# Moved words in the hand-written engine orders of a self and cross attention block

## What is computed

```python
attn_in = _adaln(x, cond, ln1_w, ln1_b, g1_w, g1_b, b1_w, b1_b)
x = _attn(attn_in, attn_in, sa_wq, sa_wkv, sa_wo, sa_bo) + x
cross_in = _adaln(x, cond, ln1_w, ln1_b, g1_w, g1_b, b1_w, b1_b)
ctx_n = _ln(context, ca_lnc_w, ca_lnc_b)
x = _attn(cross_in, ctx_n, ca_wq, ca_wkv, ca_wo, ca_bo) + x
ffn_in = _adaln(x, cond, ln2_w, ln2_b, g2_w, g2_b, b2_w, b2_b)
h = jax.nn.gelu(ffn_in @ ff_w1 + ff_b1, approximate=False)
x = h @ ff_w2 + ff_b2 + x
```

## Time and profile before

| | |
|---|---|
| times of three runs | 1933.48, 1933.77, 1937.64 us |
| the profiled execution, span of its instructions | 1934.6 us |
| TensorE (PE) busy | 1889.5 us, 98% |
| its weight loads (PEld) busy | 1289.2 us, 67% |
| VectorE (DVE) busy | 1582.3 us, 82% |
| GpSimd (POOL) busy | 1266.3 us, 65% |
| ScalarE (ACT) busy | 945.2 us, 49% |
| chain that ended last | PE 87%, POOL 4%, issue 3%, DVE 3% |

### The profile page before, as it was taken

How to read it: one execution, slowest core, us unless ns; L and a number is a source line. 1 busy time by engine, 2 the same in 40 slices (tenths; PEclk the granted TensorE clock), 3 DMA queues, 4 the chain that set the end, 5 groups by cost and what they waited for, 6 DMA issues and landing times.

```text
span 1934.6 us, 52084 instructions
## 1 busy us (share of the span) xinstructions
PE 1889.5 (98%) x19952; PEld 1289.2 (67%) x19952; DVE 1582.3 (82%) x2316; ACT 945.2 (49%) x1460; POOL 1266.3 (65%) x816
## 2 busy tenths in 40 slices
PE   7999999979999999999999999999999999999999
PEld 5666767745666666666666666666666666666664
DVE  4999999967888888888888888888888888888842
ACT  3555545533545444445554445455444445544444
POOL 4777756415776676677767677776776667667661
PEclk8999999978999999999999999999999999999999
DMA  5332233211111111111111111111111111111100
GB/s 176 117 88 86 81 112 88 73 33 48 53 54 53 55 51 53 59 55 54 54 51 55 52 58 57 51 56 51 55 50 56 57 54 56 51 53 52 53 29 23
DMA packets 147729, 119.07 MB, mean 62 GB/s; under 512 B 63392, under 2 KB 111648, under 8 KB 147488
## 3 DMA queue, kind: packets, MB, share of 16 engines
q1 hardware_dynamic: 110624, 115.46, 17.9%
q10 hardware_dynamic: 36864, 0.28, 1.0%
HBM read 36.71 MB, written 1.05 MB: 20 GB/s over the span
## 4 chain that ended last, share of the span: by engine, by line
PE 87%; POOL 4%; issue 3%; DVE 3%; DMA 1%; ACT 1%; SPq 0%; ACTq 0%; DVEq 0%; POOLq 0%
PE S L1376 24%; PE OB L1390 20%; PE PB L1338 10%; PE PB L1325 10%; PE S L1357 7%; PE PB L1399 2%; PE PB L1310 2%; PE S L1225 2%; PE PB L1409 1%; PE PB L1191 1%; PE OB L1253 1%; PE OB L1236 1%; DMA swapped<-turned 1%; POOL KL L667 1%; POOL psum_acc L674 1%
## 5 line engine op out<-in xcount | busy, mean ns | idle before, releaser
L708 POOL TENSOR_TENSOR psum_acc<-psum_acc,P 124x1024 f32<-124x1024 f32 (+1 forms) x320 | 689.8, 2156 | 216.9 <-ACT P L851 207.4
L851 ACT ACTIVATE P<-S 124x1024 f32<-124x1024 f32 (+1 forms) x448 | 431.3, 963 | 514.6 <-PE S L1376 513.9
L1069 DVE TENSOR_REDUCE mxc<-S 128x2 f32<-128x1024 f32 x384 | 470.0, 1224 | 94.9 <-PE S L1357 88.1
L1390 PE MATMUL OB<-P,V 124*64 124x256 f32 (+1 forms) x3328 | 437.3, 387 | 0.0
L1390 PEld LDWEIGHTS OB<-P,V 124*64 124x64 f32 (+1 forms) x3328 | 221.4, 137 | 188.7 <-issue 104.8
L701 POOL TENSOR_TENSOR psum_acc<-P 124x1024 f32<-124x1024 f32 x64 | 152.0, 2374 | 213.4 <-ACT P L851 213.4
L1376 PE MATMUL S<-QH,KH 64*124 64x256 f32 (+1 forms) x1664 | 271.8, 323 | 5.8 <-ACT P L851 5.8
L728 ACT ACTIVATE V<-PB 124x512 f32<-124x512 f32 (+1 forms) x320 | 157.2, 491 | 206.4 <-PE PB L1338 167.0
L1376 PEld LDWEIGHTS S<-QH,KH 64*124 64x124 f32 (+1 forms) x1664 | 154.0, 181 | 128.5 <-issue 104.7
L1376 PE MATMUL S<-QL,KH 64*124 64x256 f32 (+1 forms) x1664 | 235.2, 278 | 0.0
L1376 PE MATMUL S<-MX,share 64*124 64x256 f32 (+1 forms) x1664 | 235.0, 278 | 0.0
(11 more groups left out here) (159 smaller groups left out, 2844.8 us busy)
## 6 DMA issues: line engine op xcount, KB each, us to landing
swapped<-turned SPq DMA_DIRECT2D x512, 128.0 KB, 2.1
kv_w<-sa_kv_dram SPq DMA_DIRECT2D x64, 128.0 KB, 2.3
qswapped<-qturned SPq DMA_DIRECT2D x128, 64.0 KB, 1.9
kv_w<-ca_kv_dram SPq DMA_DIRECT2D x64, 96.0 KB, 2.2
ctxT_all<-ctx_dram SPq DMA_DIRECT2D x8, 624.0 KB, 4.4
q_w<-sa_wq_dram SPq DMA_DIRECT2D x64, 64.0 KB, 2.0
q_w<-ca_wq_dram SPq DMA_DIRECT2D x64, 64.0 KB, 2.0
o_w<-ca_wo_dram SPq DMA_DIRECT2D x64, 64.0 KB, 2.0
```

The source lines that it names most:

```text
L708: pool.tensor_tensor(acc, acc, P_of(J, c)[0:rows, :, 0:w], ALU.add).then_inc(x.acc, 1)
L851: act.activation(P_of(J, c)[0:rows, :, 0:w], SP[0:rows, :, 0:w], ACT.Exp, scale=SCALE).then_inc(x.e, 1)
L1069: dve.tensor_reduce(mxc[:, t, :, c:c + 1], MP[:, :, 0:w], AX.X, ALU.max).then_inc(x.am, 1)
L1390: ins = pe.matmul(OB[half(h), 0:N], Vb[J % 2][0:w, t, half(h)], P_of(J, c)[0:w, h, k * N:(k + 1) * N], start=(t == 0), stop=(t == len(a_.t ...
```

## The change

Only the order strings change; every instruction is there as before.

```diff
--- before.py
+++ after.py
@@ -81,20 +81,19 @@
     CTX = B * M + 56
     TOK = CTX - B * CW
     SELF = Stage("sa",
-                 "qk+3 ln+3 o+-2 p+-1 sum+-1 v+2 s a+2 ct n",
-                 "c+2 ln+2 am+1 ad+-2 r+2 t+3 rc+-1 dv+-1 cn n",
-                 "mr+1 ve+2 e ca cn ln+3 h+3 oe",
-                 "f cp l+3 cc+3 cq",
-                 "w+4 x+3")
+                 "qk+3 ln+3 o+-2 p+-1 sum+-1 v+2 a+2 s ct n",
+                 "c+2 ln+2 cn+-1 am+1 ad+-2 r+2 t+3 rc+-1 dv+-1 n",
+                 "ve+2 mr+1 e ca cn ln+3 h+3 oe",
+                 "cp l+3 f+1 cc+3 cq",
+                 "w+5 x+3")
     CROSS = Cross("ca", DC, M, 124, 512,
-                  "a4 k1+1 p2+-1 v3+-1 a5 n0 s4+-1 q+1 p3+-1 a6 s5+-1 p4+-1 v0 k2+1 n1 p5+-1 s6+-1 a0+1 v1 n2 s0 "
-                  "a1+1 p6+-1 k3+1 v2 n3 s1 a2+1 sum+-1 k0+2 n4 s2 a3+1 p0 p1 o+-1 s3",
-                  "am4 kc0+1 kt1+1 am5 qt+1 ka0+1 am6 qc+1 kl0+1 nm n0 kc1+1 ka1+1 kt2+1 kc2+1 n1 am0+1 kl1+1 ka2+1 am1+1 "
-                  "kl2+1 kt3+1 am2+1 kc3+1 rc+-1 dv+-1 ka3+1 am3+1 kl3+1 ad+-1 kt0+2",
-                  "e1+-1 e2+-1 kh3 e3+-1 ve3+-1 e4+-1 kh0+1 e5+-1 mr ve0 n0 qh+1 e6+-1 kh1+1 ve1 n1 e0 kh2+1 ve2 "
-                  "oe+-1 n2",
-                  "c4+-1 qa+1 c5+-1 cf+-1 c6+-1 ql+1 c1 c2 c3",
-                  "w+2 k0+1 k1+1 q+1 wo k2+1 k3+1")
+                  "a4 k1+1 p2+-1 v3+-1 a5 n0 s4+-1 q+1 p3+-1 a6 s5+-1 p4+-1 v0 k2+1 n1 p5+-1 s6+-1 a0+1 v1 n2 s0 a1+1 p6+-1 v2  "
+                  "k3+1 n3 s1 a2+1 sum+-1 k0+2 n4 s2 a3+1 p0 p1 o+-1 s3",
+                  "am4 kc0+1 am5 kt1+1 qt+1 ka0+1 am6 qc+1 kc1+1 kl0+1 nm n0 ka1+1 kt2+1 kc2+1 am0+1 kl1+1 ka2+1 n1 am1+1  "
+                  "kt3+1 kl2+1 am2+1 kc3+1 rc+-1 dv+-1 ka3+1 am3+1 kl3+1 ad+-1 kt0+2",
+                  "e1+-1 e2+-1 kh3 e3+-1 ve3+-1 e4+-1 kh0+1 e5+-1 mr ve0 n0 qh+1 e6+-1 kh1+1 ve1 n1 e0 kh2+1 oe+-1 ve2 n2",
+                  "c4+-1 qa+1 c5+-1 cf+-1 c6+-1 c1 c2 c3 ql+1",
+                  "k0+1 k1+1 q+1 wo w+3 k2+1 k3+1")
     assert B == PAIRS == 2 * UNROLL and LNC == 2 * N and T == GROUP * LNC
     assert all(B * M - b * (M - CW) >= 0 and (M - CW) * b + (512 - 4 * DC) * 3 <= TOK for b in range(B))
 
```

## The result

The kernel after takes 1946.99 us (median of four runs, 1946.09 to 1950.85), the kernel before 1934.62 us beside it (four runs, 1933.48 to 1937.64): a ratio of 1.0069, 95% interval 1.0053 to 1.0085, some 13 us slower. The profiled execution of after spans 1945.8 us, against 1934.6.

A forecast was written before the change was run, and what follows sets the result against it. TensorE was taken to bound cross, TensorE and VectorE nearly full in self. Self +0.3 us (0.3 + 0.5 + 0.6 - 1.1) and cross +0.5 make +0.8 on 1933.8: 1934.6 us, range 1928 to 1941.

The forecast's parts named there:

- The prediction's own sign of being wrong: Wrong if the cross period moves over 0.05 us, the waits of xT fall, or the half-clock stretches differ.
- its low ends: Whole kernel: the time with every term at its lowest bound, given as 1932 us.
- What bounds the kernel: Cross: TensorE, 22.64 us per body. Self: TensorE and VectorE nearly full, VectorE waiting 8.9 us before adds.
- Maximum scores ahead of scores: Self, TensorE: a barely hidden wait 0.3 us, later exponentials 0.5 us, later sums at the start 0.6 us.
- V's copy ahead of the rows of maxima: Self, ScalarE: copy comes 0.5 us sooner, rows leave 0.7 us later, nobody waits; 0, bounds -0.2 to +0.5 us.
- cn, fold, weights: Self: first norm's steps a body later on VectorE hide two waits, -1.1 us; GpSimd's fold and SP's weights 0.
- v2 ahead of k3: Cross, TensorE: both words take 1.10 us with k3 last against 1.09 today; value 0.
- the rival of the uncovered load: Cross, TensorE: k3 last leaves a load uncovered, 0.1 us in 61 bodies, +6.1 us, 1940.7; chance 10%.
- kt3 ahead of kl2, kc1 ahead of kl0, o, ql, weights in cross: Cross: kt3 ahead of kl2 may delay k0, +0.5 us, bounds 0 and 1.5; the others 0.
- am5 ahead of kt1: Cross, VectorE: swaps of kt1 and q leave 1 to 2 us later, GpSimd 2 us ahead of sums; no cost.
- a new wait of TensorE in cross: Cross: k0 waits for kl2, 0.3 us in half the bodies, 9 us, 1943.6, twice that in all; chance 9%.
- The clock: TensorE: one or two half-clock stretches fewer, 1927.6 to 1931, chance 12%; or more, 1938 to 1941, chance 5%.

## Why the prediction was wrong, point by point

Predicted were 1934.6 us, within 1928 to 1941; measured 1946.99. The prediction's own sign of being wrong came: the cross period moved by more than 0.05 us, from 22.64 to 22.78. (Two slips in it decide nothing: its low ends add up to 1932.9 us, not 1932, and cross attention, from 455 to 1880 us, is 74% of the time, not 70.)

*What bounds the kernel:* right. The loss is new waits of TensorE in cross and of TensorE and VectorE in self.

*Maximum scores ahead of scores:* 1.4 us predicted, 0.4 measured alone (-1.4 to +2.1), and no idle of PE ahead of the maximum scores, so the size is in keeping with both 1.4 and none. But the step gave the sums' distance to the reciprocal to this edit alone. The other edit used the same distance, and both together cost 5 us more than one by one.

*V's copy ahead of the rows of maxima:* the first step that failed. It said that of the exponentials behind the two issues "their scores end later anyway, and the issues are done by then", and set 0, at most +0.5. Measured 4.5 us alone, more with the other edit. The trace of before held the numbers: issues of 0.5 and 0.6 us that begin with V's copy, 0.75 us behind the start of V's projection, end at about 1.9, and the scores end at 1.8. Nothing was to spare, and an issue that is slow now counts in full, as in the body above where the two took 2.73 us and the table load began 0.11 us behind them. The bound of +0.5 left no room for a slow issue.

*cn, fold, weights:* the two waits of the earlier trace rows are gone; alone -0.6 us, in keeping with -1.1 and with none.

*v2 ahead of k3:* right. In the body of after at 1018.37 us v2 is followed by k3 0.87 us later and k3 takes 0.22, 1.09 us for both, where 1.10 was predicted; the rival of the uncovered load falls by these distances. The 0.06 us of a6's columns is an estimate, which the scores of the same body bear out: there two matmuls of 256 columns start every 0.12 us, which is 0.06 for four of 66. The weight loads recorded in before last 137 ns in the median for 64 columns (k's) and 192 ns for 128 (the maximum scores').

*kt3 ahead of kl2, kc1 ahead of kl0, o, ql, weights in cross:* right as far as can be told. The wait of the scores' loads for KL is 23.5 us in before and in after.

*am5 ahead of kt1:* the second step that failed. The text saw that kt1's swap and q's behind it leave "1 to 2 us later" and set 0, because GpSimd "is 2 us ahead of the sums". That is the slack of another reader. The one that counts is q's next one in the chain: swap, rotate, high part, maximum scores. Taken at the landing of q's swap, its slack in before is 2.0 us in the median body and 0.3 in the slowest (landing at 3.55, at latest 5.23, limit about 5.5), and the edit takes 1.15. Before's landings would have told of it: in 11 bodies the swap lands later than 4.38, which is 5.53 - 1.15, by 4.1 us together. That is an estimate, with the limit and the 1.15 from the kernels that ran later; measured were 10 stalled bodies and 7.2 us for the pair alone (4.8 to 9.5), since the late swaps were slower there (3.8 to 4.2 us from issue to landing in the stalled bodies but one; 3.0 to 4.1 in the late ones of before). The term stood at 0.

*The rivals:* a new wait of TensorE in cross was there, at 9% and 9 us or more, with the right size and the wrong place: at `a0` for QH, not at `k0` for KL. The clock is not it: after spends less time at half clock than before, 50.6 against 57.9 us, and is slower. (The rival's stretch of 7 us is in before's trace: of its eight stretches at half clock four last 6.83 us, three 3.3 to 3.4 and one 20.48.) The waits before the add are unchanged, 8.7 us in 12 against 8.9.

## What to carry to other kernels

Follow a word that is moved to the end of its own chain, through every DMA that is queued behind its own, and hold the delay against the slack of the slowest body, not of the median one: both losses lie in a quarter of the bodies or fewer. An issue costs the engine that makes it (0.4 to 0.6 us each here, the slow ones in before 0.9 to 1.9): put it where this engine waits anyway, never just ahead of work that others wait for. Two edits that draw on the same slack have to be priced together. To name the words that lose, run each pair alone, and then the whole change with only these pairs turned back.

## What the runs showed of the hardware

Most DMA issues take 0.4 to 0.6 us, but 71 of 1380 in before's profile take 0.9 to 1.9 us. Most of them have a transfer of instructions beside them, one that begins between 0.3 us ahead of the issue and its end: 56 of these 71, against 88 of the 1309 faster ones. In the kernel with am5 ahead only it is 42 of 47 against 59 of 1333, in after 53 of 86 against 117 of 1294. The queue q8 moves 16 KB of instructions 166 times. The DMA queues in the first half microsecond of q's issue, in the body with the stall and in the one before it (packets, MB, share):

```profile
q1 hardware_dynamic: 54, 0.11, 58.0%
q8 instruction: 1, 0.02, 18.1%
```

```profile
q1 hardware_dynamic: 66, 0.12, 65.7%
```

In 59 bodies of the kernel with am5 ahead such a transfer begins within 0.7 us ahead to 1.6 us behind q's first issue in 10, and in all 10 the swap needs over 3.0 us from issue to landing; of the other 49 two do. In before it is 10 of 12 and 1 of 47. With am5 ahead the bodies come mostly in pairs, about 228 us apart, as the transfers drift against the body: in cross they begin 10.87 us apart in the mean, and 21 such distances, 228.4 us, are about ten bodies of 22.78. After shows the same when the whole path from k1's first issue is looked at: in 26 of 62 bodies such a transfer begins 0.3 to 2.9 us behind that issue, and all 14 stalled bodies (the 13 above and the one ahead of them) are among these 26. This is a coincidence in time, shown in the traces; no run changed the transfers of instructions, so that they are the cause is likely but not shown. In before the same late swaps occur (landing at up to 5.2 instead of 3.55), and GpSimd alone waits for them, not TensorE.
